# Rows of the q and k stacks laid out feature by feature instead of part by part

## The reference

```python
# one attention of the nine that the kernel's attention segments compute (here L3_xattn)
q = (query @ Wq + bq).reshape(b, sq, NUM_HEADS, HEAD_DIM).transpose(0, 2, 1, 3)
k = (key @ Wk + bk).reshape(b, skv, NUM_HEADS, HEAD_DIM).transpose(0, 2, 1, 3)
v = (value @ Wv + bv).reshape(b, skv, NUM_HEADS, HEAD_DIM).transpose(0, 2, 1, 3)
scores = jnp.einsum('bhqd,bhkd->bhqk', q, k) * SCALE
attn = jax.nn.softmax(scores, axis=-1)
out = jnp.einsum('bhqk,bhkd->bhqd', attn, v)
out = out.transpose(0, 2, 1, 3).reshape(b, sq, D_MODEL)
...
x = _layernorm(x + _L0_attn_ref(x, ...))   # then L0 xattn, L0 ffn, L1 attn, L1 xattn, L1 ffn, L2 ..., L3 ffn
```

## Time and profile before

| | |
|---|---|
| median of 3 runs | 2792.96 us (2787.64 to 2805.41) |
| the profiled execution | 2794.28 us, its span 2792.5 us |
| mean granted clock of TensorE | 0.838 |
| PE busy | 2181.8 us |
| VectorE (DVE) busy | 1623.4 us |
| ScalarE (ACT) busy | 1197.0 us |
| GpSimd (POOL) busy | 653.5 us |
| bytes moved by DMA | 133.01 MB |

### The profile page before, as it was taken

How to read it: one execution, slowest core, us unless ns; L and a number is a source line. 1 busy time by engine, 2 the same in 40 slices (tenths; PEclk the granted TensorE clock), 3 DMA queues, 4 the chain that set the end, 5 groups by cost and what they waited for, 6 DMA issues and landing times. The chain is left out here.

```text
span 2792.5 us, 44082 instructions
## 1 busy us (share of the span) xinstructions
PE 2181.8 (78%) x15402; PEld 1103.4 (40%) x15402; DVE 1623.4 (58%) x3578; ACT 1197.0 (43%) x2187; POOL 653.5 (23%) x845
## 2 busy tenths in 40 slices
PE   2599999975799996738999888629687773768888
PEld 1133355433233443614554444228522221335556
DVE  4578766577787542345666544234567772446665
ACT  0167766642377642213666665303232211433333
POOL 4202111234211110422111111043236663100000
PEclk9699999976699995867999988659898875778898
DMA  3422221101212110622212000028500000111111
GB/s 113 97 38 27 25 36 34 33 15 17 41 24 29 25 16 9 222 41 36 34 30 40 19 17 16 13 88 281 173 0 1 0 1 24 31 46 54 53 61 46
DMA packets 106847, 133.01 MB, mean 48 GB/s; under 512 B 26007, under 2 KB 90327, under 8 KB 105988
## 3 DMA queue, kind: packets, MB, share of 16 engines
q1 hardware_dynamic: 101556, 115.32, 18.4%
q0 software_dynamic: 3776, 7.79, 0.8%
q10 hardware_dynamic: 1296, 7.08, 0.7%
HBM read 70.65 MB, written 13.49 MB: 30 GB/s over the span
## 5 line engine op out<-in xcount | busy, mean ns | idle before, releaser
L1326 ACT ACTIVATE probs<-psE 128x512 f32<-128x512 f32 (+2 forms) x1248 | 698.6, 584 | 413.4 <-PE psE L1165 224.9
L1450 DVE TENSOR_REDUCE maxima<-psM 128x2 f32<-128x1024 f32 (+4 forms) x640 | 679.2, 1082 | 335.4 <-PE psM L1142 153.3
L1165 PE MATMUL psE<-q_stack,k_stack 53*128 53x512 bf16 (+3 forms) x1152 | 367.8, 356 | 46.2 <-ACT probs L1326 29.3
L1142 PE MATMUL psM<-k_stack,q_stack 51*128 51x512 bf16 (+3 forms) x1280 | 357.3, 349 | 43.1 <-DMA k_stack<-k_parts 21.9
L1601 POOL TENSOR_SCALAR pool_t<-mean_var 128x4 f32<-128x4 f32 x60 | 15.1, 251 | 901.4 <-DVE mean_var L1387 896.7
L2298 DVE SCALAR_TENSOR_TENSOR hres<-psM,gates,hres 128x128 f32<-128x128 f32 x512 | 144.2, 344 | 84.0 <-PE psM L2232 83.1
L1165 PEld LDWEIGHTS psE<-q_stack,k_stack 53*128 53x128 bf16 x1152 | 98.5, 94 | 230.4 <-ACT probs L1326 138.4
L1142 PEld LDWEIGHTS psM<-k_stack,q_stack 51*128 51x128 bf16 x1280 | 102.2, 97 | 207.3 <-issue 130.2
L1077 PE MATMUL psM<-masks_bf,ident_bf 64*128 64x128 bf16 (+2 forms) x832 | 151.4, 264 | 29.7 <-DMA k_stack<-k_parts 24.1
L2232 PEld LDWEIGHTS psM<-values,probs 128*128 128x128 f32 x1024 | 137.9, 197 | 60.0 <-issue 59.6
L1185 PE MATMUL psB<-probs,values 128*32 128x256 f32 (+3 forms) x1696 | 155.6, 440 | 2.2 <-ACT probs L1326 1.2
(11 more groups left out here) (408 smaller groups left out, 3625.1 us busy)
## 6 DMA issues: line engine op xcount, KB each, us to landing
q_stack<-q_parts SPq DMA_DIRECT2D x432, 64.0 KB
values<-experts_dram SPq DMA_DIRECT2D x40, 514.0 KB
values<-experts_dram SPq DMA_DIRECT2D x32, 512.0 KB, 3.4
k_stack<-k_parts SPq DMA_DIRECT2D x192, 64.0 KB
hid<-experts_dram SPq DMA_DIRECT2D x15, 514.0 KB
work<-experts_dram SPq DMA_DIRECT2D x15, 514.0 KB
pack<-pack_dram SPq DMA_DIRECT2D x1, 4647.0 KB
work<-sorted SPq DMA_DIRECT2D x70, 65.0 KB
```

The lines of the kernel that those rows point to most:

```text
L1142: out, len(heads), keys, lo, max_mask(c, t), lambda i, to, start, stop: nc.tensor.matmul(to, q_stack[lo:lo + R_MAX, job.a % Q_SLOTS, pair_ ...
L1165: lambda h, to, start, stop: nc.tensor.matmul(to, ks[lo:lo + R_END, pairs[h], k * P:k * P + c.kn], q_stack[lo:lo + R_END, job.a % Q_SLOTS, ...
L1326: nc.scalar.activation(probs[0:c.kn, m % 2, heads[0]:heads[-1] + 1, q0:S], psE[0:c.kn, n % 2, 0:len(heads) * (S - q0)].rearrange("p (h q) ...
L1450: nc.vector.tensor_reduce(top, psM[:, at:at + len(banks), 0:per * keys].rearrange("p b (h k) -> p b h k", h=per), AX_X, ALU.max, negate=Tr ...
```

## The change

The rows of a stack are laid out feature by feature: part j of feature d, before in row 8 j + d, is in row 6 d + j. One transfer still moves one part of eight features and so writes rows j, 6 + j, ..., 42 + j of its half, six apart. It is the same for q and for k, so the contraction is the same sum in another order. In the planner a q move, or a k move of a wide job, costs 0.35 instead of 0.3.

```diff
--- before.py
+++ after.py
@@ -672,7 +672,7 @@
                 moves = task in ("q_move", "k_move")
                 n = 1 if moves else 2 if x.job.att.wide else 4
                 free[engine] = at + 0.06 * n
-                queue = max(queue, free[engine]) + (0.1 if not moves else 0.3 if task == "q_move" or x.att.wide else 0.08)
+                queue = max(queue, free[engine]) + (0.1 if not moves else 0.35 if task == "q_move" or x.att.wide else 0.08)
                 end = queue + 1.7
             elif engine == "NONE":
                 end = at
@@ -1612,6 +1612,9 @@
 
                 @block.sync
                 def _(sp):
+                    def part_rows(j, hb):
+                        return slice(64 * hb + j, 64 * hb + NB * (DH - 1) + j + 1, NB)
+
                     def slot_free(job, before):
 
                         if before[job]:
@@ -1622,17 +1625,15 @@
                         if task == "q_move":
                             i = item[2]
                             j, hb = divmod(i, 2)
-                            lo = 64 * hb + DH * j
                             if i == 0:
                                 sp.wait_ge(q_split, split_no["q_split"][job])
                                 slot_free(job, before_q)
-                            sp.dma_start(q_stack[lo:lo + DH, job.a % Q_SLOTS, :, :],
+                            sp.dma_start(q_stack[part_rows(j, hb), job.a % Q_SLOTS, :, :],
                                          q_parts[64 * hb:64 * hb + 64, (0, 0, 0, 1, 1, 2)[j], :])\
                                 .then_inc(q_moved[job.a % Q_SLOTS], 16)
                         elif task == "k_move":
                             i, nk = item[2], job.att.nk
                             j, hb = divmod(i, 2)
-                            lo = 64 * hb + DH * j
                             ks, _ = k_side(job)
                             if i == 0:
                                 sp.wait_ge(k_split, split_no["k_split"][job])
@@ -1643,7 +1644,7 @@
                                         sp.dma_start(ks[at:at + 3, :, 0:nk],
                                                      src.unsqueeze(1).to_broadcast([3, H // 2, nk]))\
                                             .then_inc(k_moved(job), 16)
-                            sp.dma_start(ks[lo:lo + DH, :, 0:nk],
+                            sp.dma_start(ks[part_rows(j, hb), :, 0:nk],
                                          k_parts[64 * hb:64 * hb + 64, (0, 1, 2, 0, 1, 0)[j], 0:nk])\
                                 .then_inc(k_moved(job), 16)
                         elif task == "rows_evac":
```

## The result

| | before | after |
|---|---|---|
| median of 4 runs each | 2799.18 us (2787.64 to 2808.04) | 2758.82 us (2757.07 to 2764.77) |
| ratio | | 0.9868, 95% interval 0.9835 to 0.9901 |
| the profiled execution's span | 2792.5 us | 2755.4 us |
| mean granted clock | 0.838 | 0.846 |
| share of the 16 engines that the moves' queue took | 18.4% | 14.0% |

The kernel is 1.3% faster, where 1.1% was forecast. The ratio and its interval are those on record; the quotient of the two medians alone would be 0.9856. What the trace shows agrees with the forecast in the first half of its argument, and not in the second. These lines of the page of after answer to the earlier trace rows; the second is the DMA queue of the moves, with packets, MB and the share of time, and the last is the same queue in before.

A forecast was written before the change was run, and what follows sets the result against it. TensorE bounds the kernel (busy 78%), so only its stalls for moves count: 24.1 us at three wide starts, 6 at the maxima, 1 at the narrow start, 31 us off the 2792.96 us median, giving 2762 us; range 2745 to 2775.

The forecast's parts named there:

- The pace of a burst: In bursts of 24 q moves, a move takes SP's own 0.65 us instead of 1.0 us; bounds 0.65 and 1.0.
- The tail behind the last issue: At a wide start, PE begins its first score 1.85 us after SP's last issue ends, instead of 9.9 us.
- the three wide starts: First score, L1a's start and second segment's start come 8.0, 7.9 and 8.2 us sooner; 24.1 us in sum.
- The waits for the maxima: Row transfers behind each second burst lose 9.0 us of excess wait in all; two thirds counted, 6 us.
- The narrow start: Last segment's start, q moves alternating with 9.6 KB moves: 0.5 us gained, 1 us with one or two later jobs.
- rows that share a way in: Write side of the moves: adjacent target rows share a way in, so spreading eight rows over 43 removes the 65 GB/s limit.
- (a): Rival on move rate: it belongs to rows or streams, not where rows lie; time stays 2793 us; chance 0.16.
- (b): Rival on the moves' writes: a spread write is slower than a dense one, 1.17 us a move, 2812 us; chance 0.05.
- One sign that was named: The second segment's start was to come 10 to 20 us earlier than its own burst explains.
- It is kept to the end ... what follows moves forward as a block: After the three wide starts, their 24.1 us lead lasts to the end, since every queue has a fixed order.
- rival (c): Planner order: bursts are faster, but the new cost swaps items, three to five swaps of 3 us; 2775 us; chance 0.11.
- upside: Elsewhere in attention phases PE's work hides the moves; without that cover each 24-move burst would be worth up to 8 us.

The follow-up runs named there:

- e4: Transfer-only kernel, no decoder work: ten phases of 14 queued transfers at different target row spacings; four adjacent rows 27 GB/s, eight 55, six apart 91 and 93.
- e1: The changed kernel with the planner's old move cost 0.30: new rows, old order of tasks; 2756.11 us, ratio 0.9846.
- e9: As e1, with eleven tiny transfers ahead of the first k move to hold the first burst back; 2762.24 us, ratio 0.9871.
- e2: The kernel before with the planner's move cost at 0.35: old rows, new order of tasks; 2814.68 us, ratio 1.0042.
- e6: Padded: new rows in the old order, with 56 dummy matmuls before the first score and the first job's scores doubled; 2777.27 us, ratio 0.9905.
- e5: Padded: the kernel before, with 92 dummy matmuls ahead of the first score and the first job's scores doubled; 2818.12 us, ratio 1.0056.
- e3: The changed kernel with the first segment planned at move cost 0.30 (old order), the others at 0.35; 2740.21 us, ratio 0.9787.
- e10: The changed kernel with planner move cost 0.65 in the first two segments and 0.35 in the last; 2741.36 us, ratio 0.9797.

## Why the prediction was right, and where it only came out right

**Right, step by step.** The pace of a burst is SP's 0.65 us (100 GB/s for 65). The tail behind the last issue was put at 1.85 us and is 1.77, 1.84 and 1.83; the three wide starts land 8.1, 7.9 and 8.2 us sooner behind their issue, against 8.0, 7.9 and 8.2. The waits for the maxima are gone: 4.33, 3.72 and 4.99 us from issue to use became 1.19, 1.19 and 1.41. The narrow start is 0.6 us, of 0.5 put down. The reason given, rows that share a way in, was shown by e4. Rivals (a) and (b) are out. One sign that was named did not come: the second segment was to start 10 to 20 us earlier than its own burst explains, and in after it starts 8.8 us earlier, 0.6 more than its burst. In e1 it starts 23.7 us earlier, 15.5 more; the order had taken the difference in L1a and L1c.

**"It is kept to the end ... what follows moves forward as a block": this step failed for the first start.** The lead of e1 over before on ScalarE is 6.7 us at the first start, 9.75 at 110 us and -0.8 at 172 us. It went into the half clock, which e1 is granted from 91.0 to 162.7 us without a break, while before has the full one in three stretches of that time (0.59 against 0.72, above); in e9 a start 6.8 us later ends no later. In the new order 8.6 of the 9.0 us between e2 and after are kept (0.70 in both). The leads of the two later starts were kept: with the rows alone PE is 11.5 us ahead at the first score of L1a and 13.5 at the end of segment 1, 23.7 at the start of segment 2 and 38.7 at its end. The prediction drew on the clock in mid-segment alone, where it was 1.00, though it is at 0.50 and 0.55 in the first burst.

**"The new planner cost swaps items ... three to five swaps of 3 us" (rival (c)): the mechanism is real and its size was wrong.** It was given a chance of 0.11 and a price of 13 us. The order costs 20 us in L1a and L1c alone, 12 in the whole with the old rows, and some 6 with the new ones, which is not clear of noise, and most of the 20 us are PE at work at a lower clock, not a transfer that comes 3 us late. Pricing it by one visible wait on SP had nothing to do with that.

**The term that was too small: segment 2.** 2.4 us of its maxima were counted (two thirds of 3.65); its stretch lost 15.1 us with the rows alone, 10.0 in the padded pair. The prediction held that elsewhere everything is hidden by PE's work, from a window of 20 us, and named the rest as upside. 11.4 of the 15.1 us are PE's own busy time at a higher clock.

**The term with the wrong sign: segment 3.** 0.5 to 1 us of gain were counted for the narrow start. The start itself gave 0.6, but behind it the new rows in the old order are slower: 445.4, 445.5 and 445.6 us to the end (e1, e6, e9), against 439.7 and 439.6 with the old rows (before, e5). PE is busy 351.3 us (e1) instead of 343.7, at a clock of 0.80 for 0.82. In the new order the rows gain there instead (437.1 in after, 443.0 in e2). The prediction had no term for this.

So 31 us were forecast for the rows and nothing for the order. The rows gave 43 us (1.54% of 2800), the order took some 6 back, and 37 to 40 remain. The number stood in part by luck: a head start that was lost, a segment that gained more and an order that cost partly cancelled, and the range held it for the same reason. That 2762 us lies so near to 2758.82 also owes something to the start of the sum: 2792.96 us was the median of three runs, and with the fourth it is 2799.18.

## What to carry to other kernels

Where a transfer writes few rows, set them four or more apart (4, 6, 8 and 16 did equally well here), and look for the need of it where the last packet lands many us after the last issue, with a rising DMA share at a falling GB/s. After any change of a latency, plan the order anew for each part of the kernel and measure it: here a planner number chosen for each segment brought 0.7 to 0.8% on top of the change's 1.3%, and its truth was no guide. A head start of a few us in a stretch where PE's clock is not at its full level may be worth nothing; read the granted clock of the stretch behind it before counting it.

## What the runs showed of the hardware

- With 14 transfers queued, four adjacent target rows take 27 GB/s and eight 55 (e4). When successive transfers go to other rows the same eight-row writes reach 71 to 73 GB/s: they overlap in part. Spacings of 4, 6, 8 and 16 rows are alike, 91 to 96 GB/s, at SP's pace.
- The granted clock has two levels here, 0.50 and 1.00, and the same sequence of matmuls was given one or the other according to how it fell in time. From the first score to the third copy of `o_raw` it was 0.72 (before), 0.59 (e1), 0.58 (e3, the same rows and order) and 0.67 (e9, as e1 but held back 6.8 us). That is 92.2, 100.0, 101.5 and 91.8 us for the same work. Why the full level comes at one moment and not 7 us sooner, none of the runs settles.
- The pattern can repeat closely: from the first score of segment 3 to the end, which begins with PE idle for 18 to 20 us, kernels with the same rows and order in this segment agree to 0.2 us (439.6 and 439.7; 445.4 to 445.6; 437.0 and 437.1), though what came before differs by tens of us. e10, again with the rows and order of after here, has 435.3, so it isn't a rule.
